# A two-layer graph kernel: statistics of two rows in one instruction, the mean taken off on GpSimd, the hidden layer of the edge weights computed in a stage of its own

## The chip, the cores and the metric

The kernel runs on one core of a Trainium2 chip. The metric is the device time of one execution in microseconds (us), without a profiler. The engines are TensorE (PE), VectorE (DVE), ScalarE (ACT), GpSimd (POOL) and SyncE (SP), which only issues transfers. Each runs its own instructions in order, and they wait for each other on semaphores.

## What is computed

100,000 nodes have 160 features each (64 scalars and 32 vectors of three), and 25,000 edges, sorted by their target, carry messages. Two layers follow each other, each with a layer norm and a ReLU ahead of it:

```python
h = jnp.maximum(_layernorm(x, axis=-1), 0.0)
x = x + L0(h, node_vec1, edge_attr_4, edge_attr_8, weights, src, dst)
h = jnp.maximum(_layernorm(x, axis=-1), 0.0)
x = x + L1(h, edge_attr_4, weights, edge_index)
```

In L0 every node gets a linear map of its own h, scaled by cos(angle). Every edge takes the mapped h of its source, times weights that a small network makes of the edge's 8 scalars, and the sums of the edges at a node go through a second map and are scaled by sin(angle). The small network is the part that the change moves:

```python
h = jax.nn.silu(edge_scalars @ fc_w1 * (1.0 / np.sqrt(8.0)))
weight = h @ fc_w2 * (1.0 / np.sqrt(64.0))
```

L1 gathers the rows of the sources again, forms messages, sums them per node, and adds the ReLU of a linear map of the sum. The layer norm's scale 1/sqrt(var + eps) is positive, so that the kernel takes the ReLU of x - mean first and multiplies by the scale later, behind the matmul.

## The kernel before

There are three stages behind a start of some 70 us, in which tables of the edges are computed and stored to DRAM.

**Stage 1** has 98 steps (u), one for each *unit* of 1024 nodes (8 rows in each of the 128 partitions). A step also handles two *tiles* of 128 edges; four tiles are a *quad* (q), so there are 49 quads of two steps each, an even one and an odd one. For a unit, DVE takes the statistics of the rows (`dense_stats`, L1334), forms mean and variance in small instructions (`moment_part`, L1203 to L1210) and takes the mean off 32 of the 160 columns (`rest_of`, L1215). ACT takes it off the other 128 with the ReLU (`dense_relu`, L763), PE transposes (L964, L965), ACT copies from PSUM (L770, L771), PE multiplies (`linear`, L969, L970), DVE scales and adds x (`dense_x1`, L1353) and takes the second statistics (L1362), ACT forms the second h (L755), and POOL adds it to x (`dense_y`, L625). POOL also computes the inverse roots by a power (`inverse_root`, L628). For a quad, POOL gathers the source rows with four indirect DMAs (L581), PE and ACT compute the hidden layer (`net_mm`, L1025; `net_silu`, L775), and DVE builds two selector matrices from a table of rows (`p1_selectors`, L1374). For a tile, PE multiplies (`p1_source`, ends with L1057), ACT copies (L802), DVE forms features (L1421, L1426, L1430), PE transposes them (L1083) and multiplies (L1043 to L1046), DVE forms the message (L1402, L1409), and PE sums (L1069, L1071).

SP's loop is a list of steps of its own (v). Step v loads the rows of unit v (`x_load`, L428). Even steps then load the source index (L443) and the edge scalars `q_sct` (L445) of quad v/2 + 1, and odd steps load the tables of quad (v-1)/2: `q_key`, `q_ed`, `q_row` (L450 to L452). Each step then stores the results of unit v-4 (L436, L438). DVE needs the tables of quad q at the end of its odd step 2q-1, so that SP has to be two steps ahead of DVE there.

**Stage 2** computes the 25,000 target rows again, with the edge sums, and scatters them to DRAM: per quad four indirect gathers and four indirect scatters on POOL, on DVE the same moments, an angle in eight small steps, and on ACT a Sine and two Square roots, which don't share a table. **Stage 3** handles layer L1's 196 tiles, with one indirect gather and one indirect scatter for each.

Of the kernel before, what the change touches and what calls it, by code (L numbers as in the profile page):

```python
# [19 lines left out]
P = 128  # L20
GD = 8
GQ = 4
# [52 lines left out]
def gnn_kernel(nc, xa, src, dst, number, edges_in, scalars_in, scalars_t_in, wpack, out):  # L75
# [19 lines left out]
    sum_tab = scratch("sum_tab", (Q, P, GQ * CW))  # L95
    y_tab = scratch("y_tab", (Q, P, GQ * D))
# [23 lines left out]
    with ExitStack() as ctx:  # L120
# [34 lines left out]
        minus_half = sb("minus_half", [P, GD])  # L155
# [21 lines left out]
        st1, st2 = four("st1", [P, GD, 6]), two("st2", [P, GD, 6])  # L177
        su1, su2 = four("su1", [P, GD, 2]), two("su2", [P, GD, 2])
        df1, df2 = four("df1", [P, GD]), two("df2", [P, GD])
        sq1, sq2 = four("sq1", [P, GD]), two("sq2", [P, GD])  # L180
        m21, m22 = four("m21", [P, GD]), two("m22", [P, GD])
        neg1, neg2 = four("neg1", [P, GD]), two("neg2", [P, GD])
        var1, var2 = four("var1", [P, GD]), two("var2", [P, GD])
# [16 lines left out]
        q_sct = two("q_sct", [GQ * SW, P])  # L200
# [5 lines left out]
        hr_e = two("hr_e", [P, GQ * 32])  # L206
# [9 lines left out]

        x_q = [x_all[:, i * GQ * XW:(i + 1) * GQ * XW] for i in range(4)]
# [4 lines left out]
        st_e = two("st_e", [P, GQ, 6])  # L222
        su_e = two("su_e", [P, GQ, 2])
        df_e = two("df_e", [P, GQ])
        sq_e = two("sq_e", [P, GQ])
        m2_e = two("m2_e", [P, GQ])
        neg_e = two("neg_e", [P, GQ])
        var_e = two("var_e", [P, GQ])
        sd_e = two("sd_e", [P, GQ])
        sd2 = two("sd2", [P, GQ])  # L230
# [38 lines left out]
        n_act = sem("net_hidden_ready")  # L269

        d_in = [sem(f"x_loaded{i}") for i in range(4)]
        d_ln1 = sem("dense_moments1")
        d_relu = sem("dense_h_ready")
# [6 lines left out]
        d_ln2 = sem("dense_moments2")  # L280
        d_h1 = sem("dense_h1_ready")
# [5 lines left out]
        e_tb = sem2("p1_tables_loaded")  # L287
        e_scl = sem("p1_scale_ready")
        e_g = sem2("p1_source_rows")
        e_ln = sem("p1_moments")  # L290
        e_relu = sem("p1_h_ready")
# [27 lines left out]
        r_relu = sem("p2_h_ready")  # L319
# [31 lines left out]
        def x3(t, w, g):  # L351
            return t[:, :].rearrange("p (g f) -> p g f", g=g, f=w)

# [14 lines left out]
        def _(sp):  # L368
# [53 lines left out]
            sp.wait_ge(s_rows, 32)  # L422
            sp.wait_ge(s_tab_out, 16 * n_out)
# [143 lines left out]
        def _(pool):  # L567
            nc.gpsimd.memset(t_next[:, :], N + 5).then_inc(s_fill, 1)
            nc.gpsimd.memset(t_prev[:, :], -1).then_inc(s_fill, 1)
            nc.gpsimd.memset(minus_half[:, :], -0.5)  # L570
# [40 lines left out]
            def p1_gather(q):  # L611
                j = q.mod(2)
                pool.wait_ge(e_ix[j], q.over(2, 16, 16))
                wait(pool, e_relu, q.times(1, -1))
                wait(pool, e_scl, q.times(2, -2))
                gather(xa, x_e[j], XW, i_src[j], e_g[j])
# [10 lines left out]
            def inverse_root(inv, var, n, signal):  # L627
                nc.gpsimd.tensor_tensor(inv[:, 0:n], var[:, 0:n], minus_half[:, 0:n], ALU.pow).then_inc(signal, 1)  # L628

            def dense_scale(u):  # L630
                j = u.mod(4)
                pool.wait_ge(d_ln1, u.times(5, 4))
                inverse_root(inv1[j], var1[j], GD, d_scl)
                pool.wait_ge(d_scl, u.times(2, 1))
                nc.gpsimd.tensor_tensor(scl1[j][:, :], inv1[j][:, :], x3(x_in[j], XW, GD)[:, :, D], ALU.mult).then_inc(d_scl, 1)

            def dense_norm2(u):
                j = u.mod(2)
                pool.wait_ge(d_ln2, u.times(4, 4))
                inverse_root(inv2[j], var2[j], GD, d_nmr)  # L640
                pool.wait_ge(d_nmr, u.times(2, 1))
                nc.gpsimd.tensor_tensor(nmr2[j][:, :], neg2[j][:, :], inv2[j][:, :], ALU.mult).then_inc(d_nmr, 1)  # L642

            def p1_scale(q):
                j = q.mod(2)
                pool.wait_ge(e_ln, q.times(5, 4))
                inverse_root(inv_e[j], var_e[j], GQ, e_scl)
                pool.wait_ge(e_scl, q.times(2, 1))
# [3 lines left out]
            def step(w):  # L652
                q = At(w.i, w.c // 2, 2)
                if w.mod(2) == 1 and (q + 1).within(Q):
                    p1_gather(q + 1)
                if (w - 1).within(U):
                    dense_scale(w - 1)
                if (w - 4).within(U):
                    dense_y(w - 4)
                if (w - 3).within(U):  # L660
                    dense_norm2(w - 3)
                if w.mod(2) == 0 and q.within(Q):
                    p1_scale(q)
# [3 lines left out]
            for w in range(8):  # L667
                step(At(0, w))
            with pool.Fori(2, U // 4) as i:
                for c in range(4):  # L670
                    step(At(i, c))
            for w in range(U - 2, U + 4):
# [74 lines left out]
        def _(act):  # L747
# [11 lines left out]
            def dense_relu(u, h):  # L759
                act.wait_ge(d_ln1, u.times(5, 3))  # L760
                x, hh = x_in[u.mod(4)], hb[u.mod(2)]
# [1080 lines left out]
```

## Time and profile before

| | us |
|---|---|
| Device time, median of three runs | 2476.07 (2475.62 to 2479.8) |
| Profiled execution, first to last instruction | 2863.6 |
| of it start, to 73 | 73 |
| stage 1, 73 to 1505 (49 quads) | 1432 |
| stage 2, 1505 to 2190 (49 quads) | 685 |
| stage 3, 2190 to 2863 (196 tiles) | 673 |

The profiled execution is 387 us longer than the kernel without a profiler. It is one execution, and each stage has a bound of its own: shares of the whole span say little. Durations of rows overlap a little: the next instruction of an engine can start before the one ahead is recorded as ended, so that the cost of one in a row of several is the distance of their starts.

### The profile page before, as it was taken

The numbers are of one execution on the slowest core, as the hardware profiler recorded it, in microseconds if no ns is written. First come the engines' busy times: TensorE is split into PE (matmuls) and PEld (weight loads), VectorE is DVE, ScalarE is ACT, GpSimd is POOL, SyncE is SP. The second block draws the span as 40 slices with busy tenths as digits, with TensorE's granted clock in tenths as the row PEclk, the third lists the DMA queues.
The fourth block names the chain that finished last, engine by engine and source line by source line (L and its number), as shares of the span: only waits on it lengthen the run. The fifth ranks groups of instructions, "written<-read, shape, count | busy, mean of one in ns | idle before, by whom it ended". The sixth has DMA issues, their size and how long they took to land.

```text
span 2863.6 us, 55863 instructions
## 1 busy us (share of the span) xinstructions
PE 1940.9 (68%) x12874; PEld 1820.7 (64%) x12874; DVE 1954.7 (68%) x8628; ACT 1560.1 (54%) x4412; POOL 1745.2 (61%) x1676
## 2 busy tenths in 40 slices
PE   0888888878878888878883343434344777777877
PEld 0777777777877777777773333323233777767777
DVE  2889888887888888888884655556555444444444
ACT  0667677776777777777774444545453222222222
POOL 1656666665666666766656565655565666666665
PEclk9989999998999999999995555555555999999898
DMA  9444544443444444454543232323332333333332
GB/s 79 142 143 169 172 170 171 172 172 138 169 172 170 173 169 164 162 179 147 180 154 124 87 89 87 93 87 97 88 99 83 81 89 88 92 92 90 94 95 74
DMA packets 223602, 364.52 MB, mean 127 GB/s; under 512 B 115938, under 2 KB 133149, under 8 KB 223405
## 3 DMA queue, kind: packets, MB, share of 16 engines
q1 hardware_dynamic: 176524, 289.81, 32.1%
q0 software_dynamic: 47040, 74.31, 9.8%
q14 instruction: 27, 0.21, 0.0%
q8 instruction: 11, 0.18, 0.0%
HBM read 176.85 MB, written 194.78 MB: 130 GB/s over the span
## 4 chain that ended last, share of the span: by engine, by line
DVE 31%; PE 25%; issue 14%; another core or an unknown queue 11%; POOL 8%; ACT 6%; SPq 2%; DMA 1%; DVEq 1%; ACTq 0%; POOLq 0%
DVE st L1334 3%; PE bank L969 3%; PE bank L1154 3%; POOL x_e L581 3%; POOL inv L628 3%; DVE x L1353 2%; DVE su_e L1203 2%; PE bank L964 2%; PE bank L1166 2%; DVE st L1362 2%; PE bank L1163 2%; ACT h L755 2%; PE bank L1176 2%; DVE x L1599 2%
## 5 line engine op out<-in xcount | busy, mean ns | idle before, releaser
L628 POOL TENSOR_TENSOR inv<-var,minus_half 128x8 f32<-128x8 f32 x196 | 327.7, 1672 | 256.5 <-DVE var L1210 253.4
L625 POOL TENSOR_TENSOR yo<-x,h 128x640 f32<-128x640 f32 x196 | 305.8, 1560 | 147.8 <-ACT h L755 145.4
L969 PE MATMUL bank<-wp,hT 128*128 128x160 f32 x1568 | 392.6, 334 | 1.6 <-DVE x L1353 0.7
L755 ACT ACTIVATE h<-x,nmr,inv 128x160 f32<-128x160 f32 x784 | 342.2, 514 | 6.1 <-POOL nmr L642 6.1
L587 POOL DMA_INDIRECT h_all<-h,i_put x196 | 203.4, 1038 | 217.9 <-ACT h L871 146.0
L964 PE MATMUL bank<-ident,h_e 128*128 128x128 f32 x392 | 83.0, 350 | 358.9 <-ACT h_e L878 229.2
L587 POOL DMA_INDIRECT out<-yo,i_put x196 | 202.1, 1031 | 197.2 <-DVE feat L1706 63.8
L1353 DVE SCALAR_TENSOR_TENSOR x<-bank,scl,x_all 128x160 f32<-128x160 f32 x784 | 254.3, 372 | 89.1 <-PE bank L970 46.0
L969 PE MATMUL bank<-wp,eT 128*128 128x160 f32 x784 | 274.5, 444 | 54.5 <-ACT eR L886 27.3
L934 ACT ACTIVATE tot<-bank 128x160 f32<-128x160 f32 x196 | 59.6, 304 | 455.7 <-remote 207.1
L964 PEld LDWEIGHTS bank<-ident,h_e 128*128 128x128 f32 x392 | 57.5, 184 | 367.9 <-DVE hr_e L1215 244.1
L1715 DVE TENSOR_TENSOR xr<-bank,q_ed 128x96 f32<-128x96 f32 x196 | 50.0, 255 | 334.0 <-PE bank L1166 175.6
L970 PEld LDWEIGHTS bank<-wp,hR 128*128 128x128 f32 x1568 | 268.4, 199 | 0.0
L970 PE MATMUL bank<-wp,hR 128*128 128x64 f32 x1568 | 268.4, 254 | 0.0
L581 POOL DMA_INDIRECT x_e<-in_xa,i_src x192 | 192.0, 1000 | 109.5 <-issue 48.0
L969 PEld LDWEIGHTS bank<-wp,hT 128*128 128x128 f32 x1568 | 253.0, 202 | 3.1 <-DVE x L1353 0.9
L763 ACT ACTIVATE hb<-x_all,neg 128x128 f32<-128x128 f32 x784 | 248.7, 394 | 0.0
L719 POOL DMA_INDIRECT h<-h_all,i_src x196 | 202.3, 1032 | 61.9 <-issue 58.4
L581 POOL DMA_INDIRECT x_all<-in_xa,i_dst x196 | 194.5, 992 | 65.6 <-issue 58.4
L1154 PE MATMUL bank<-ident,feat 128*128 128x128 f32 x784 | 136.1, 301 | 136.2 <-DVE feat L1706 109.8
L969 PEld LDWEIGHTS bank<-wp,eT 128*128 128x128 f32 x784 | 171.3, 270 | 73.8 <-issue 46.5
L964 PE MATMUL bank<-ident,hb 128*128 128x128 f32 x784 | 131.7, 294 | 117.7 <-ACT tot L810 115.9
(173 smaller groups left out, 6292.4 us busy)
## 6 DMA issues: line engine op xcount, KB each, us to landing
x_all<-in_xa SPq DMA_DIRECT2D x98, 644.0 KB, 5.8
h_all<-h SPq DMA_DIRECT2D x98, 640.0 KB, 2.9
out<-yo SPq DMA_DIRECT2D x98, 640.0 KB, 3.3
q_row<-row_tab SPq DMA_DIRECT2D x98, 256.0 KB
sum_tab<-tot SPq DMA_DIRECT2D x49, 322.0 KB, 4.2
y_tab<-yo SPq DMA_DIRECT2D x49, 320.0 KB
x<-y_tab SPq DMA_DIRECT2D x49, 320.0 KB
cv<-sum_tab SPq DMA_DIRECT2D x25, 322.0 KB
```

Source lines behind the costliest of these rows:

```text
L581: nc.gpsimd.indirect_dma_start(into[:, t * width:(t + 1) * width], None, rows, bass.IndirectOffsetOnAxis(ap=index[:, t:t + 1], axis=0)).th ...
L587: nc.gpsimd.indirect_dma_start(rows, bass.IndirectOffsetOnAxis(ap=index[:, t:t + 1], axis=0), tile, None, bounds_check=N - 1, oob_is_err=F ...
L625: nc.gpsimd.tensor_tensor(yo[j][:, a:b], x1[j][:, a:b], h1[j][:, a:b], ALU.add).then_inc(d_y, 1)
L628: nc.gpsimd.tensor_tensor(inv[:, 0:n], var[:, 0:n], minus_half[:, 0:n], ALU.pow).then_inc(signal, 1)
L719: nc.gpsimd.indirect_dma_start(h1[j][:, t * D:(t + 1) * D], None, h1_all, bass.IndirectOffsetOnAxis(ap=i_src[j][:, t:t + 1], axis=0)).then ...
L755: ins = nc.scalar.activation(h1[j][:, k * D:(k + 1) * D], x1[j][:, k * D:(k + 1) * D], ACT.Relu, bias=nmr2[j][:, k:k + 1], scale=inv2[j][: ...
L763: ins = nc.scalar.activation(hh[:, k * P:(k + 1) * P], x[:, k * XW + 32:k * XW + D], ACT.Relu, bias=neg1[u.mod(4)][:, k:k + 1])
L964: nc.tensor.transpose(ps_main[:, t * P:(t + 1) * P], main[:, t * P:(t + 1) * P], ident[:, :])
L969: nc.tensor.matmul(dst_ps, main[:, t * P:(t + 1) * P], wp[:, w:w + D], start=True, stop=False)
L970: return nc.tensor.matmul(dst_ps[:, 0:DS], rest[:, :], wp[:, w + D + t * DS:w + D + (t + 1) * DS], start=False, stop=True)
L1154: ins = nc.tensor.transpose(bank[n.mod(2)][:, c * P:(c + 1) * P], feat[n.mod(2)][:, c * P:(c + 1) * P], ident[:, :])
L1353: ins = V.scalar_tensor_tensor(x1[j][:, k * D:(k + 1) * D], bank[2 + pair % 2][:, k % 2 * D:(k % 2 + 1) * D], scl1[u.mod(4)][:, k:k + 1], ...
```

## The change

Four things are changed.

1. **Statistics.** One `bn_stats` instruction reads two rows, interleaved, and so puts out count, mean and squared deviation of each; the small instructions that joined the halves are gone. The roots are taken on ACT in stage 1 (for the nodes), with a reciprocal on DVE; for the edges POOL keeps its power.
2. **Mean.** The mean is taken off all 160 columns on POOL in stage 1 (`centre`), for a unit in an instruction of 1024 columns and one of 256, for a quad in one of 512 and one of 128. In stage 2 DVE does it.
3. **ReLU.** ACT's copy from PSUM applies it, and ACT's own instructions for it are gone.
4. **Hidden layer.** It is computed for all quads ahead of stage 1, in 13 groups of up to four quads, and stored to DRAM (`hid_tab`). In stage 1 SP loads it per quad, in the place of the scalars.

```diff
-    for k in range(GD):
-        ins = V.bn_stats(st1[j][:, k, :], x_in[j][:, k * XW:k * XW + D])
+    for pair in range(GD // 2):
+        ins = paired_stats(st1[j], pair, x_in[j], XW)
...
+def paired_stats(st, pair, rows, width):
+    two_rows = rows[:, 2 * pair * width:(2 * pair + 2) * width].rearrange("p (g f) -> p f g", f=width)
+    return V.bn_stats(st[:, 2 * pair:2 * pair + 2, :].rearrange("p g k -> p (g k)"), two_rows[:, 0:D, :])
...
+def centre(into, rest, rows, st, g, signal):
+    x = x3(rows, XW, g)
+    nc.gpsimd.tensor_tensor(x3(into, P, g), x[:, :, 32:D], bc_last(stat(st, g, 1), P), ALU.subtract)
+    nc.gpsimd.tensor_tensor(x3(rest, 32, g), x[:, :, 0:32], bc_last(stat(st, g, 1), 32),
+                            ALU.subtract).then_inc(signal, 1)
...
 def dense_copy(u, h):
-    nc.scalar.activation(hT[h][:, :], bank[0][:, :], ACT.Copy)
+    nc.scalar.activation(hT[h][:, :], bank[0][:, :], ACT.Relu)
...
 def p1_load(q):                       # SP
     j = q.mod(2)
     wait(sp, e_g[j], q.over(2, 64))
     sp.dma_start(i_src[j][:, :], src_tab[q.times(1)]).then_inc(e_ix[j], 16)
-    wait(sp, n_mm, q.times(1, -1))
-    sp.dma_start(q_sct[j][:, :], scalars_t[q.times(1)]).then_inc(n_in[j], 16)
+    wait(sp, e_pw, q.times(GQ, -GQ))
+    sp.dma_start(q_hid[j][:, :], hid_tab[q.times(1)]).then_inc(e_hid[j], 16)
...
+net_load(0)                            # SP, ahead of stage 1
+for g in range(NB):
+    if g + 1 < NB:
+        net_load(g + 1)
+    net_store(g)
+for j in range(2):
+    sp.wait_ge(n_st[j], 16 * ((NB + 1 - j) // 2))
```

The SP queue in the loop of stage 1: the end of an even step and the odd step behind it. `net_products_done` is the semaphore that `net_mm` counts, `p1_products_done` the one that `p1_source` counts, once for each tile. Before:

```order
L445 ISA [waits net_products_done]
L445 DMA q_sct<-scalars_t 32x128
L435 ISA
L436 ISA [waits dense_h1_ready]
L436 DMA h_all<-h 128x1280
L438 DMA out<-yo 128x1280 [waits dense_y_ready]
...
L428 DMA x_all<-in_xa 128x1288
...
L450 DMA q_key<-key_tab 128x8
...
L452 DMA q_row<-row_tab 128x512
```

In the changed kernel:

```order
L465 ISA [waits p1_products_done]
L465 DMA q_hid<-hid_tab 128x256
L455 ISA
L456 ISA [waits dense_h1_ready]
L456 DMA h_all<-h 128x1280
L458 DMA out<-yo 128x1280 [waits dense_y_ready]
...
L448 DMA x_all<-in_xa 128x1288
...
L470 DMA q_key<-key_tab 128x8
...
L472 DMA q_row<-row_tab 128x512
```

The transfers and their order are the same but for the hidden layer in the scalars' place; the wait ahead of it is another.

The POOL queue in the same loop. `inv`, `scl` and `nmr` are a unit's inverse root, its product with the node's attribute and the shift of the second norm, `yo` is the sum of x and h, and `hb` and `hr` are the rows less their mean. Before, the first step of the loop:

```order
L628 TENSOR_TENSOR inv<-var,minus_half 128x8 [waits dense_moments1]
...
L635 TENSOR_TENSOR scl<-inv,x_all 128x8 [waits dense_scale_ready]
...
L625 TENSOR_TENSOR yo<-x,h 128x640 [waits dense_out_stored0]
...
L625 TENSOR_TENSOR yo<-x,h 128x640 [waits dense_h1_ready]
...
L628 TENSOR_TENSOR inv<-var,minus_half 128x8 [waits dense_moments2]
```

In the changed kernel:

```order
L602 DMA x_e<-in_xa,i_src 128x161 [waits p1_centred]
L602 DMA x_e<-in_xa,i_src 128x161 x3
...
L649 TENSOR_TENSOR hb<-x_all,st 128x1024 [waits dense_h_transposed]
L650 TENSOR_TENSOR hr<-x_all,st 128x256
...
L645 TENSOR_TENSOR yo<-x,h 128x640 [waits dense_out_stored1]
...
L645 TENSOR_TENSOR yo<-x,h 128x640 [waits dense_h1_ready]
```

The roots have left POOL, two wide instructions stand ahead of the sums, and the gather has moved to the front of the even step.

## Rows read from the trace of the kernel before

**Rows 1.** Busy time by stage: busy us (x instructions), then clock, DMA share, GB/s

```profile
73.00:1505.00 1432.00, 1163.77 (x8272) 1096.56 (x8272) 1226.07 (x5217) 1034.31 (x3073) 928.50 (x871) 0.93 0.47 164
1505.00:2190.00 685.00, 262.50 (x1030) 234.90 (x1029) 398.23 (x2257) 338.69 (x745) 400.01 (x394) 0.52 0.31 93
2190.00:2863.00 673.00, 508.66 (x3528) 485.38 (x3528) 315.22 (x1078) 183.83 (x588) 407.21 (x395) 0.90 0.34 88
```

**Rows 2.** The chain that ended last, its shares by engine over the whole span

```profile
DVE 31%; PE 25%; issue 14%; another core or an unknown queue 11%; POOL 8%; ACT 6%; SPq 2%; DMA 1%; DVEq 1%; ACTq 0%; POOLq 0%
```

**Rows 3.** Timeline of POOL in stage 2: start, duration, instruction, [idle before]

```profile
1833.66 0.94 POOL L581 DMA_INDIRECT x_all<-in_xa,i_dst  x1 [0.30 <-issue]
1837.50 1.00 POOL L587 DMA_INDIRECT h_all<-h,i_put  x1 [0.30 <-issue]
```

**Rows 4.** Line L789, once in a quad: durations, first and last start

```profile
L789 ACT ACTIVATE eT<-bank x49: 597/597/597, 72.6 to 1465.9; 128x512 f32<-128x512 f32 x49
```

**Rows 5.** Groups by line and form: busy us, mean ns, idle before and releaser

```profile
L625 POOL TENSOR_TENSOR yo<-x,h 128x640 f32<-128x640 f32 x196 | 305.8, 1560 | 147.8 <-ACT h L755 145.4
L770 ACT ACTIVATE hT<-bank 128x512 f32<-128x512 f32 x196 | 117.0, 597 | 135.1 <-PE bank L965 133.5 <-issue 1.6
```

**Rows 6.** Timeline of POOL and DVE in an even step of stage 1

```profile
815.26 1.53 POOL L625 TENSOR_TENSOR yo<-x,h 128x640 f32<-128x640 f32 x1 [0.61 <-ACT h L755]
815.39 1.42 DVE L1206 TENSOR_SCALAR neg_e<-su_e 128x4 f32<-128x4 f32 x1
```

**Rows 7.** Busy time in stretches of 5 us in stage 1, columns as in rows 1

```profile
1110.00:1115.00 5.00, 3.87 (x31) 3.41 (x29) 3.68 (x16) 4.20 (x12) 3.57 (x4) 1.00 0.57 174
1120.00:1125.00 5.00, 4.38 (x19) 4.00 (x18) 4.12 (x13) 1.45 (x5) 1.18 (x1) 0.50 0.00 0
```

**Rows 8.** Timeline around a quad's selectors: SP, PE, DVE

```profile
817.43 0.35 SPq L428 DMA_DIRECT2D x_all<-in_xa  x1
819.46 0.33 SPq L452 DMA_DIRECT2D q_row<-row_tab  x1
828.15 0.95 PE L1057 MATMUL bank<-wp,q_hid 128*128 128x192 f32 x2
830.96 0.68 DVE L1374 TENSOR_TENSOR same<-q_row,q_key 128x512 f32<-128x512 f32 x1
```

**Rows 9.** Transfers of stage 1: count, KB each, median us from issue to landing

```profile
x_all<-in_xa SPq DMA_DIRECT2D x94, 644.0 KB, 5.8
sum_tab<-tot SPq DMA_DIRECT2D x48, 322.0 KB, 4.2
i_src<-src_tab SPq DMA_DIRECT2D x46, 2.0 KB, 5.2
```

**Rows 10.** Timeline of DVE and PE in stage 1, pieces of a step

```profile
817.39 1.25 DVE L1353 SCALAR_TENSOR_TENSOR x<-bank,scl,x_all 128x160 f32<-128x160 f32 x4
820.66 1.90 DVE L1334 BATCH_NORM_STATS2 st<-x_all 128x6 f32<-128x160 f32 x8
817.17 0.55 PE L1083 MATMUL bank<-ident,feat 128*128 128x128 f32 x3 [2.58 <-DVE feat L1430]
820.40 0.63 PE L964 MATMUL bank<-ident,hb 128*128 128x128 f32 x4 [0.59 <-ACT tot L810]
822.90 0.61 PE L964 MATMUL bank<-ident,h_e 128*128 128x128 f32 x4
851.59 0.61 PE L964 MATMUL bank<-ident,h_e 128*128 128x128 f32 x4
853.25 0.52 PE L1083 MATMUL bank<-ident,feat 128*128 128x128 f32 x3 [0.95 <-ACT eR L790]
```

**Rows 11.** Start: SP's last table store; a hidden layer on PE; transfers of 0:100

```profile
62.53 0.38 SPq L419 DMA_DIRECT2D row_tab<-t_row  x1
805.58 0.71 PE L1025 MATMUL bank<-q_sct,wp 32*128 32x128 f32 x4
q_sct<-scalars_t SPq DMA_DIRECT2D x4, 16.0 KB, 2.3
```

More of the change, by code:

```diff
@@ L205, in gnn_kernel @@
         h_e = sb("h_e", [P, GQ * P])
[L206 removed]
+        hr_e = sb("hr_e", [P, GQ * 32])
         part2 = two("part2", [P, GQ * D])
@@ L653, in step @@
                 q = At(w.i, w.c // 2, 2)
-                if w.mod(2) == 1 and (q + 1).within(Q):
[L655 to L663, printed above, removed]
+                if w.mod(2) == 0 and (q + 1).within(Q):
+                    p1_gather(q + 1)
+                if w.within(U):
+                    dense_centre(w)
+                if (w - 3).within(U):
+                    dense_y(w - 3)
+                if w.mod(2) == 1 and (q + 1).within(Q):
+                    p1_centre(q + 1)
+                    p1_scale(q + 1)
             pool.wait_ge(s_tab_in, 80)
             gather(xa, x_e[0], XW, t_src, e_g[0])
-            for w in range(8):
+            p1_centre(At(0, 0, 2))
+            p1_scale(At(0, 0, 2))
+            for w in range(4):
                 step(At(0, w))
-            with pool.Fori(2, U // 4) as i:
+            with pool.Fori(1, U // 4) as i:
                 for c in range(4):
                     step(At(i, c))
-            for w in range(U - 2, U + 4):
+            for w in range(U - 2, U + 3):
                 step(At(0, w))
@@ L831, in step @@
                 odd = u.mod(2) == 1
+                if (u - 2).within(U):
+                    dense_root2(u - 2)
                 if u.within(U):
-                    dense_relu(u, 0)
+                    dense_root1(u)
                 slot(u, 0)
-                if not odd and (q + 1).within(Q):
-                    net_silu(q + 1)
-                if odd and (q + 1).within(Q):
-                    p1_relu(q + 1)
                 if u.within(U):
@@ L851, in step @@
                     dense_h1(u - 2, 1)
-            net_silu(At(0, 0, 2))
-            p1_relu(At(0, 0, 2))
+            for g in range(-(-Q // GQ)):
+                net_silu(g)
             p1_copy(At(0, 0, 2))
@@ L873, in p2_h1 @@
                 ins.then_inc(r_h1, 1)
-            def p2_relu(q):
-                act.wait_ge(r_ln1, q.times(5, 3))
-                for t in range(GQ):
-                    ins = nc.scalar.activation(h_e[:, t * P:(t + 1) * P], x_q[q.mod(4)][:, t * XW + 32:t * XW + D],
-                                               ACT.Relu, bias=neg_e[q.mod(2)][:, t:t + 1])
-                ins.then_inc(r_relu, 1)
             def p2_copy(q):
@@ L1093, in slot @@
                 if (s - 1).within(T):
-                    p1_feat_t(s - 1, q1 if u.mod(2) == 0 and h == 1 and q1.within(Q) else None)
+                    p1_feat_t(s - 1)
                 if (s - 2).within(T):
@@ L1102, in step @@
             def step(u):
-                q = At(u.i, u.c // 2, 2)
-                odd = u.mod(2) == 1
                 slot(u, 0)
-                if not odd and (q + 1).within(Q):
-                    net_mm(q + 1)
                 if u.within(U):
@@ L1114, in _ @@
             pe.wait_ge(e_z, 1)
-            net_mm(At(0, 0, 2))
+            for g in range(-(-Q // GQ)):
+                net_mm(g)
+            pe.wait_ge(n_act, 2 * -(-Q // GQ))
             p1_tr(At(0, 0, 2))
@@ L1439, in step @@
                 rows = u.mod(2) == 0 and q1.within(Q)
+                odd = u.mod(2) == 1 and q1.within(Q)
                 if now:
                     dense_x1(u - 1, 0)
+                if (u - 2).within(U):
+                    dense_inverse2(u - 2)
+                if now:
                     dense_x1(u - 1, 1)
+                if (u - 2).within(U):
+                    dense_shift2(u - 2)
+                if now:
                     dense_stats2(u - 1, 0)
```

300 lines of the change are left out of this document (129 added, 171 removed).

## The prediction

> **What bounds the kernel now.** I read the stages first, since the shares of the whole span mix them. In [rows 1], stage 1 takes 1432 of 2863 us and keeps DVE busy for 1226 and PE for 1164; stages 2 and 3 take 685 and 673 us with no engine over 76%. The chain of waits [rows 2] gives DVE 31% and PE 25%, and 11%, 315 us, to a source that none of the kernel's work explains. Most of that sits in stages 2 and 3, and the profiled execution is 387 us longer than the median: I take those gaps for the profiler's own. What bounds these two stages without it is POOL's queue. An indirect transfer occupies it for 0.94 or 1.00 us and 0.30 to the next [rows 3], 1.27 on average. Stage 2 has eight per quad, 49 x 8 x 1.27 = 498 us, stage 3 two for each of 196 tiles, another 498; with filling and draining, some 1010 together. The median then leaves 2476 - 73 - 1010 = 1393 us for stage 1, **28.4 us per quad**. The trace has (1465.9 - 72.6)/48 = 29.0 [rows 4]. The median is the time that I sum against, and 28.4 is how it divides; against the span, the same differences would stand on 2863.6.
>
> **What the change takes out of stage 1, per quad.** *ACT* loses 16 of the rows' ReLUs and four for the edges, 20 x 0.3 (a copy of 512 columns has 0.6 [rows 5], these have 128), 6 us, and gains four roots of 0.2. It is off the path in most steps. *DVE* loses 36 statistics instructions for 18; eight take 1.90 [rows 10], 0.23 each, of which some 0.17 are its 160 columns at one per cycle; a pair as one instruction saves about 0.06, 1.1 us in all. The lower bound for the new one is 0.23, if two interleaved rows went at double rate, the upper 0.5 or more, if the stride cost something; I take 0.39, since nothing in the trace shows strided columns to be slower. It also loses 33 small instructions, some 3.2 us, and gains eight, 0.6. And it loses a stall: `neg_e` has four columns and took 1.42 us, ending with POOL's sum that started just ahead of it [rows 6]; there are two of these in most quads, 2.4 us. DVE is lighter by 6 of some 25 us. *PE* loses the hidden layer, 0.6 us [rows 11], but at that place it covers a wait of 0.59 for ACT's copy [rows 10], so that nothing is won. *POOL* trades its roots for wide differences: a sum of 640 columns takes 1.56 [rows 5], so 1280 columns take some 3.1 us per unit; with the edges' 640 and their scale the quad's POOL work stays at 21 us, gather included. Bounds for the 1280 columns: 2 us, if a broadcast operand is cheaper, 6 if twice as dear; 3.1 is by the nearest row, the same instruction.
>
> If nothing else changed, the longest loop would be POOL's: from DVE's statistics of an odd unit through difference (3.1), sum (3.1), the edges' difference and scale (3.3), gather (5.8), difference (3.1) and half a sum (1.5) back to DVE, and 4.9 there: 24.8 us; PE needs 23 to 24 with its unavoidable waits. Such loops ran 28.4 where the engines' sum was 25, so some 26.5 would come of it.
>
> **A wait that is added.** SP's `p1_load(q+1)` in its even step now waits until `p1_source` is through with quad q-1, since the buffer `q_hid` is read until then. Before, it waited for a product finished long before. The wait ends when PE has done its second tile of step 2q-1. Queued behind it on SP are the stores of unit 2q-4, the load of unit 2q+1 and the **tables of quad q**, which DVE needs for the selectors at the end of the same step 2q-1. [Rows 8] show the distance: `q_row` was issued at 819.46 and the selectors began at 830.96, 11.5 us later, hence without a wait. But `p1_source`, whose last product is L1057, ended at 828.15 + 0.95 = 829.1, 1.9 us ahead of the selectors. In the changed kernel the seven transfers start only there. From that end to the issue of `q_row`: from `x_all` to `q_row` it is 2.0 us [rows 8], and `q_hid` and two stores ahead take 0.5 each with the wake-up, 3.9 in all. The data wait behind 2 MB: the load of x lands 5.8 us after its issue, and even 2 KB issued behind it take 5.2 [rows 9]. `q_row` lands between 3.9 + 2.3 = 6.2 us (small loads of the start [rows 11]) and 10 us (x at 1.9 + 5.8, its own 256 KB and the stores ahead). I take 9.0, nearer to [rows 9], since these stand in the same queue.
>
> The quad is then a ring. After the landing: selectors 1.2; DVE's first half of a step 3.4 (817.39 to 820.66 [rows 10], less the pair's gain, plus two small ones), the next unit's statistics 1.6, two pairs of `x1` 1.2, statistics 1.6, features and message 1.2, small ones 0.2 and one stall behind POOL's difference, 1.0: 10.2. Then PE, by starts in [rows 10]: features to the next transposes 3.2 (817.17 to 820.40), these and the products 2.5 (to 822.90), the edges' transposes with ACT's copy 1.7 (851.59 to 853.25), and to the end of `p1_source` 2.1: 9.5. Sum 9.0 + 1.2 + 10.2 + 9.5 = 29.9. In the ring PE idles for some 2 us behind the tables. The granted clock fell to 0.50 in 1120:1125 after such a gap [rows 7], with 1.00 shortly before; I add 0.6. **30.5 us per quad, 49 x (30.5 - 28.4) = +103 us.** Bounds: 27 with the earliest landing and no loss, 33 with the latest and a fall of the clock in each quad.
>
> **The stage of its own.** SP's queue is full of table stores until 62.5 [rows 11], and the loads come behind them: nothing hides the stage. For a group, PE has two products of 512 columns. Four records of 128 columns took 0.71 [rows 11], and four of 512 take at least 2 us, twice that at the lower clock. The loop of two groups on the same buffers goes over a store (322 KB landed in 4.2 us [rows 9]; these are 512), the load behind it, a product and a copy of 0.6 [rows 5]: 7.5, or 3.7 per group. 12.25 groups are 46 us, and filling and the last store, less what stood there before, add 2: **+48 us** (30 if only PE counts, 67 if load and store follow each other).
>
> **Stages 2 and 3.** In stage 2 the statistics shrink and DVE takes the mean off 160 columns, where ACT did 128. Both lie beside POOL's eight transfers, 10.2 us per quad, against 8.3 for DVE's quickest. If that cover were gone, DVE would be the bound and lighter by a microsecond. I count nothing, and in the profile some tens of microseconds less, since fewer instructions wait for a semaphore there. Stage 3 is untouched.
>
> Sum: 2476 + 103 + 48 = 2627; I say **2625 us**.
>
> **Rivals.** *A. The ring above*: 2625. *B. The tables come in time*, and the lighter engines count: 26.5 per quad, -93 + 48, **2431 us**. It needs a landing after 5 us (21.5 + 5), below my lower bound, or PE to run further ahead of DVE than the 1.9 us of [rows 8]. For it: in other quads PE led by as little, but DVE becomes lighter, not PE, which speaks against. It is even with the kernel before at 27.4 per quad, a landing after 5.9 us; the low end of A, 27, is already past that point. *C. The port that POOL and DVE share.* The stall of [rows 6] is the mechanism: POOL would be in such an instruction for 15 of 26 us in longer pieces (2.4 us), and DVE has some nine instructions with two SBUF operands in a quad, at about 0.6 each 5 us, of which my sum has 1 in the path. With the ring, 2.5 more per quad: 33, 49 x 4.6 + 48, **2749 us**. The Trainium skill states the rule (SBUF — State Buffer, Who interferes with whom): a DVE instruction with two SBUF inputs and a GpSimd one that reads SBUF exclude each other for their whole length; by that rule the trace agrees, 1.42 us against the 0.16 of its like. *D. The change does less than it says*: two interleaved rows cost as much as two instructions. That is 1 us per quad in DVE's part, inside the range.
>
> **How the numbers follow.** A 0.65, of it 0.05 at its low end where it is faster and 0.05 within the bound; C 0.16; B 0.19. A measurement can tell some 0.2%, 5 us, so a result within that of 2476 means no change. Faster 0.24, same 0.05, slower 0.71. The range takes in B's upper half and C up to its middle: 2435 to 2730.
>
> **What would show it.** In the profile after: DVE idle ahead of the selectors on `q_row`, once per quad, some 7 us (if not, A falls); `q_row` issued behind the end of the tile's last product; quads of some 30 us; a stretch of 45 to 50 us between table stores and the first step with PE, ACT and SP in it; DVE's busy share in stage 1 down from 86% to about 65%; POOL's differences at 2.4 and 0.7 us. Quads of 26 to 27 us would make the prediction wrong, and so would stages 2 and 3 that change without the profiler.

## The result, and the profile after

| | median us (runs) | profiled span |
|---|---|---|
| before | 2477.94 (2475.62 to 2483.44) | 2863.6 |
| after | 2717.62 (2716.09 to 2722.42) | 2715.7 |

The ratio is 1.0973, with a 95% interval of 1.0955 to 1.0991: the changed kernel is 240 us slower. The profiled execution of after took what its runs take, so its rows can be read as they stand; that of before had been 387 us longer than its runs. First the stages, in the columns of [rows 1].

```profile
115.00:1650.00 1535.00, 1183.08 (x8080) 1103.32 (x8080) 1216.29 (x3130) 816.96 (x2251) 870.82 (x831) 0.91 0.45 160
1650.00:2187.00 537.00, 269.69 (x1068) 241.83 (x1069) 362.03 (x1537) 291.00 (x547) 411.48 (x397) 0.55 0.40 117
2187.00:2715.00 528.00, 451.07 (x3491) 443.91 (x3489) 314.89 (x1065) 181.59 (x580) 396.96 (x381) 0.95 0.40 108
```

Stage 1 has grown. Stages 2 and 3 look 290 us shorter than in [rows 1], but only because those carried the gaps of one execution; what they cost in runs is measured below. The line that answers [rows 4], and the chain of waits that answers [rows 2]:

```profile
L814 ACT ACTIVATE eT<-bank x49: 597/597/597, 112.3 to 1598.4; 128x512 f32<-128x512 f32 x49
...
PE 28%; DMA 16%; issue 16%; DVE 16%; SPq 8%; ACT 7%; POOL 6%; DVEq 1%; POOLq 0%; ACTq 0%
```

The first quad starts at 112.3 instead of 72.6, and quads follow each other at (1598.4 - 112.3)/48 = 31.0 us. In the chain DVE fell from 31% to 16% and DMA rose from 1% to 16%. Three groups of the page say where to look (busy us, mean ns, idle before and its releaser):

```profile
L649 POOL TENSOR_TENSOR hb<-x_all,st 128x1024 f32<-128x1024 f32 x98 | 187.7, 1915 | 465.2 <-DVE st L1210 464.1
L1427 DVE TENSOR_TENSOR feat<-feat,q_ed 128x96 f32<-128x96 f32 x196 | 296.6, 1513 | 0.0
L1379 DVE TENSOR_TENSOR same<-q_row,q_key 128x512 f32<-128x512 f32 x98 | 68.0, 693 | 322.2 <-DMA q_row<-row_tab 322.1
```

The selectors wait for `q_row`. The 322 us of the page take in stage 3; stage 1 alone has this:

```profile
L1379 DVE TENSOR_TENSOR same<-q_row,q_key x49: 681/692/694, 120.0 to 1602.8; 128x512 f32<-128x512 f32 x49
...
  DMA q_row<-row_tab: 249.1, 48
```

Of these 249 us 82 stand once at the start, which leaves 3.5 per quad. And L1427, a product of 96 columns, takes 1513 ns on average. In the kernel before, its like took 269.

**The ring**, on SP, PE and DVE (it answers [rows 8]):

```profile
818.97 0.54 PE L1069 MATMUL bank<-wp,q_hid 128*128 128x192 f32 x2
...
819.69 0.33 SPq L465 DMA_DIRECT2D q_hid<-hid_tab  x1
...
821.32 0.78 SPq L448 DMA_DIRECT2D x_all<-in_xa  x1
...
824.35 0.44 SPq L472 DMA_DIRECT2D q_row<-row_tab  x1
...
829.74 0.69 DVE L1379 TENSOR_TENSOR same<-q_row,q_key 128x512 f32<-128x512 f32 x1 [3.72 <-DMA q_row<-row_tab]
```

PE ends `p1_source` at 819.5, SP wakes at 819.7, and with the two stores and the load of x in front `q_row` is issued at 824.35. The selectors begin at 829.74, 10.2 us after PE's end; over 45 quads of stage 1 the median is 10.4.

**A hold**, on POOL and DVE (it answers [rows 6]):

```profile
820.43 1.93 POOL L649 TENSOR_TENSOR hb<-x_all,st 128x1024 f32<-128x1024 f32 x1
822.30 0.63 POOL L650 TENSOR_TENSOR hr<-x_all,st 128x256 f32<-128x256 f32 x1
822.89 3.01 POOL L645 TENSOR_TENSOR yo<-x,h 128x640 f32<-128x640 f32 x2
...
820.75 5.28 DVE L1427 TENSOR_TENSOR feat<-feat,q_ed 128x96 f32<-128x96 f32 x1
```

L1427 reads two tensors from SBUF. Begun 0.3 us after POOL's centring, it ends with POOL's run of four instructions, at 826.0. About one in four is caught so (mostly 5.3 to 6.1 us), the others take 0.24. The Trainium skill (SBUF — State Buffer, Who interferes with whom) lets such a DVE instruction and a reading GpSimd instruction exclude each other for one instruction's length; here the trace goes further, since the wait lasts through four.

**The stage of its own**, on SP and PE:

```profile
59.22 0.38 SPq L418 DMA_DIRECT2D row_tab<-t_row  x1
...
62.65 7.16 PE L1040 MATMUL bank<-yo,wp 32*128 32x512 f32 x8 [43.61 <-DMA yo<-scalars_t]
70.44 7.19 PE L1040 MATMUL bank<-yo,wp 32*128 32x512 f32 x8 [0.63 <-DMA yo<-scalars_t]
...
110.91 1.12 PE L979 MATMUL bank<-ident,h_e 128*128 128x128 f32 x4 [0.37 <-ACT x L806]
```

Two groups (eight records) come every 7.8 us, 3.9 per group. PE is busy for 7.2 of it and waits 0.6 for the load, so that PE bounds the stage.

So there were three candidates for 240 us: the ring, the hold and the stage, and one unknown, how the runs of before divide between the stages.

### The profile page after: what moved, and what is told of

The parts are those of the page before. It is cut to its first block, busy times and chain, and to the rows that moved or that the text cites. A ratio compares the mean times of both kernels' runs of the same rounds, so it can differ in the third digit from the quotient of the medians.

```text
span 2715.7 us, 51496 instructions
## 1 busy us (share of the span) xinstructions
PE 1953.1 (72%) x12730; PEld 1807.0 (67%) x12730; DVE 1906.1 (70%) x5786; ACT 1308.1 (48%) x3409; POOL 1687.4 (62%) x1628
## 4 chain that ended last, share of the span: by engine, by line
PE 28%; DMA 16%; issue 16%; DVE 16%; SPq 8%; ACT 7%; POOL 6%; DVEq 1%; POOLq 0%; ACTq 0%
DMA q_row<-row_tab 10%; PE bank L984 5%; DVE feat L1427 4%; POOL h_all L608 3%; ACT h L777 3%; DMA x_all<-in_xa,i_dst 3%; DVE st L1210 3%; PE bank L1093 2%; PE bank L985 2%; PE bank L979 2%; DVE x L1353 2%; DMA out<-yo,i_put 2%; PE bank L1069 2%; POOL x_all L602 2%; PE bank L1056 2%
## 5 line engine op out<-in xcount | busy, mean ns | idle before, releaser
L649 POOL TENSOR_TENSOR hb<-x_all,st 128x1024 f32<-128x1024 f32 x98 | 187.7, 1915 | 465.2 <-DVE st L1210 464.1
L984 PE MATMUL bank<-wp,hT 128*128 128x160 f32 x1568 | 403.1, 341 | 12.9 <-DVE x L1353 12.3
L645 POOL TENSOR_TENSOR yo<-x,h 128x640 f32<-128x640 f32 x196 | 298.8, 1532 | 98.1 <-ACT h L777 98.0
L1427 DVE TENSOR_TENSOR feat<-feat,q_ed 128x96 f32<-128x96 f32 x196 | 296.6, 1513 | 0.0
L1379 DVE TENSOR_TENSOR same<-q_row,q_key 128x512 f32<-128x512 f32 x98 | 68.0, 693 | 322.2 <-DMA q_row<-row_tab 322.1
L1353 DVE SCALAR_TENSOR_TENSOR x<-bank,scl,x_all 128x160 f32<-128x160 f32 x784 | 254.1, 365 | 17.0 <-PE bank L985 16.3
L1093 PE MATMUL bank<-ident,feat 128*128 128x128 f32 x588 | 110.0, 299 | 205.4 <-DVE feat L1427 157.6
L608 POOL DMA_INDIRECT h_all<-h,i_put x196 | 215.3, 1098 | 61.5 <-issue 58.6
L798 ACT ACTIVATE hT<-bank 128x512 f32<-128x512 f32 x196 | 117.0, 597 | 226.6 <-PE bank L980 226.6
L1093 PEld LDWEIGHTS bank<-ident,feat 128*128 128x128 f32 x588 | 67.8, 153 | 228.4 <-DVE feat L1427 170.5
L1210 DVE BATCH_NORM_STATS2 st<-x 128x6 f32<-128x320 f32 x490 | 218.0, 485 | 0.0
```

Of the source, the lines that this page charges most:

```text
L608: nc.gpsimd.indirect_dma_start(rows, bass.IndirectOffsetOnAxis(ap=index[:, t:t + 1], axis=0), tile, None, bounds_check=N - 1, oob_is_err=F ...
L645: nc.gpsimd.tensor_tensor(yo[j][:, a:b], x1[j][:, a:b], h1[j][:, a:b], ALU.add).then_inc(d_y, 1)
L984: nc.tensor.matmul(dst_ps, main[:, t * P:(t + 1) * P], wp[:, w:w + D], start=True, stop=False)
L1093: ins = nc.tensor.transpose(bank[4][:, c * P:(c + 1) * P], f[:, at:at + P], ident[:, :])
L1210: return V.bn_stats(st[:, 2 * pair:2 * pair + 2, :].rearrange("p g k -> p (g k)"), two_rows[:, 0:D, :])
L1353: ins = V.scalar_tensor_tensor(x1[j][:, k * D:(k + 1) * D], bank[2 + pair % 2][:, k % 2 * D:(k % 2 + 1) * D], scl1[u.mod(4)][:, k:k + 1], ...
```

## The experiments

All times are medians beside runs of the kernel before on the same chip (2480 to 2486 us). "Pace" is the start of the 49th `same` less that of the first, over 48, in the profile of that run. "Rest" is the median less the start of the 49th.

| kernel | us | ratio to before (95%) | pace | rest |
|---|---|---|---|---|
| before, stage 1 only | 1424.6 | | 27.2 | |
| after | 2717.6 | 1.097 (1.096 to 1.099) | 30.9 | 1115 |
| after, `q_hid` loaded behind the tables | 2693.5 | 1.086 (1.084 to 1.088) | 30.1 | 1132 |
| after, no two SBUF inputs in features | 2747.0 | 1.108 (1.106 to 1.110) | 31.3 | 1123 |
| after, both | 2523.7 | 1.018 (1.016 to 1.020) | 26.8 | 1119 |
| before + stage and its wait | 2825.0 | 1.138 (1.135 to 1.141) | 33.3 | 1106 |
| before + stage, `q_hid` behind the tables | 2528.6 | 1.020 (1.018 to 1.021) | 27.1 | 1109 |
| hidden layer in the loop | 2604.8 | 1.051 (1.048 to 1.054) | 29.6 | 1115 |
| the same, no two SBUF inputs in features | 2476.4 | 0.998 (0.997 to 0.999) | 26.9 | 1118 |
| and selectors ahead of `dense_stats` | 2419.2 | 0.973 (0.971 to 0.975) | 25.7 | 1111 |
| and selectors while POOL gathers | 2400.9 | 0.965 (0.962 to 0.968) | 25.2 | 1120 |
| in the loop, gather between centre and sum | 2417.7 | 0.973 (0.971 to 0.974) | 25.5 | 1121 |
| in the loop, features mended, gather last | 2559.3 | 1.030 (1.028 to 1.033) | 28.6 | 1115 |

**1. How before divides.** On every engine all that follows stage 1 is left out, so that nodes with edges lack the second layer.

```diff
-    p2_step(...) and p3_slot(...) with their loops, on SP, POOL, ACT, PE and DVE
+    SP waits for the last stores of h, out and sum_tab
```

> The kernel before with stages 2 and 3 left out (the rows of touched nodes get no second layer). It gives the time of the start and stage 1 without a profiler. The prediction's split (73 us of start, 28.4 per quad) gives about 73 + 1393 + 12 for the last stores: about 1475 us. The split by the profile after (stages 2 and 3 cost 1100 us there) gives 2478 - 1100 = about 1380 us, 26.6 per quad.

1424.6 us, between the two. Its profiled span is 1422.5, 2 us less than its run, so that it has none of the gaps that made the profile of before longer:

```profile
L1067 DVE TENSOR_TENSOR same<-q_row,q_key x49: 675/680/693, 71.0 to 1374.6; 128x512 f32<-128x512 f32 x49
```

Stage 1 of before runs at 27.2 us per quad and not at 28.4. Behind the 49th selectors 2480 - 1375 = 1105 us follow, in all other kernels 1106 to 1132: the change does little to stages 2 and 3, some 10 us more.

**2. The wait, in the changed kernel.**

```diff
     i_src load
-    wait(sp, e_pw, ...); q_hid load      # p1_load(q + 1), even step
 ...
     q_key, q_ed, q_row loads             # p1_tables(q), odd step
+    wait(sp, e_pw, ...); q_hid load      # for q + 1
```

> The changed kernel, except that SyncE issues the load of q_hid for the next quad behind the three table loads of this quad, instead of ahead of them. Theory W (the wait on e_pw, with the tables queued behind it, sets the pace of stage 1: 30.9 us per quad in the profile after against about 26.6 without it): 48 quads get 4.3 us back, 2717 - 206 = about 2510 us. Theory P (GpSimd's centring holds up VectorE's feature instructions, 1513 ns for the 96-column one against 269, and that sets the pace): the pace stays near 30, 2670 us or more.

Only 24 us came back (2693.5). By itself that would speak for theory P.

**3. The stage and its wait in the kernel before.** Statistics, ReLUs and roots stay as they were.

```diff
-    net_mm(q + 1), net_silu(q + 1)       # in the even step of PE and ACT
+    net_mm(g), net_silu(g)               # all groups ahead of the first step
-    wait(sp, n_mm, ...); q_sct load      # p1_load(q + 1)
+    wait(sp, e_pw, ...); q_hid load
```

> The kernel before with the hidden layer alone changed: computed in a stage of its own, q_hid loaded by SyncE behind the same wait on e_pw; statistics, mean and ReLU as before. Theory W: it gets the wait and the stage, so 2478 + 43 for the stage + about 4.3 x 48 = 206: about 2725 us, or a little more since VectorE's half of the ring is longer in this kernel. Theory P: no centring on GpSimd, so nothing but the stage: 2478 + 43 = about 2520 us.

2825.0: 345 us slower, more than the whole change. The pace went to 33.3, and every selector waited:

```profile
L1400 DVE TENSOR_TENSOR same<-q_row,q_key x48: 691/692/693, 119.0 to 1691.3; 128x512 f32<-128x512 f32 x48
...
  DMA q_row<-row_tab: 431.9, 48
```

Its counterpart has the same stage with `q_hid` behind the tables:

> The kernel before with the hidden layer in a stage of its own, but q_hid loaded by SyncE behind the table loads, so that no table waits for e_pw. No centring on GpSimd. If the wait is the whole of what before plus the stage lost besides the stage itself: 2480 + 43 = about 2525 us (2505 to 2545). If reading q_hid from memory or the later start of the loop costs something else: 2600 us or more.

2528.6. The wait alone, without any centring on POOL, is 2825 - 2529 = **296 us**, and the stage alone **47 us**. The selectors have no wait but the one at the start:

```profile
L1406 DVE TENSOR_TENSOR same<-q_row,q_key x49: 676/681/693, 116.8 to 1419.8; 128x512 f32<-128x512 f32 x49
...
  DMA q_row<-row_tab: 78.7, 1
```

**4. The statistics without the stage.** The changed kernel with two products and one SiLU per quad in the loop, as before; the diff is that of experiment 3 with + and - exchanged.

> The changed kernel with the hidden layer back in the loop (two products and one SiLU per quad, inputs loaded by SyncE behind n_mm) and no stage of its own; statistics, centring, ReLU in the copy and roots as in the changed kernel. Theory W: no wait and no stage, so the time of before or a little less for VectorE's and ScalarE's 6 us per quad: 2430 to 2480 us. Theory P: the centring on GpSimd alone makes a quad dearer by 3 to 5 us: 2620 to 2700 us.

2604.8: 125 us slower than before with no wait and no stage. That is theory P's outcome, 15 us below the near end of its 2620 to 2700: both theories hold. Its features, written without two SBUF inputs:

```diff
-    tensor_tensor(f[128:320], w[128:192] (x3), g[64:160], mult)
+    tensor_tensor(f[128:224], w[128:160] (x3), g[64:160], mult)
 ...
-    tensor_tensor(f[224:320], f[224:320], ed(j, t, 1, 4), mult)
+    for i in range(3):      # w is in PSUM, the scalar is a column
+        scalar_tensor_tensor(f[224 + i::3], w[160:192], ed(j, t, 1 + i, 2 + i), g[64 + i::3], mult, mult)
```

> The changed kernel with the hidden layer back in the loop, and VectorE's features written so that no instruction of them reads two tensors from SBUF: the 96-column product feat x q_ed becomes three products of 32 columns (PSUM x a column of q_ed x g_e), and the 192-column product becomes one of 96. Theory P (an instruction with two SBUF inputs is held until GpSimd's run of centring and addition ends, once per quad, 5.3 us, and PE waits 2.9 us of it for the features and 1.2 behind that): with the hold gone 2.9 to 4.1 us x 48 come back, 2605 - 140 to 195 = 2410 to 2465 us. Theory L (the centring is simply one more step between statistics and transposes, and its latency sets the pace): 2580 us or more.

2476.4: the hold had cost 128 us here, 2.7 per quad, where PE's waits in the profile had led me to expect 2.9 to 4.1. The 128 us include what a lower clock cost, see below.

**5. Both causes, taken apart in the changed kernel.**

> The changed kernel whole (the stage, the wait on e_pw ahead of the tables), with the features written without two SBUF inputs. If the ring through q_row holds the pace by itself, as in before plus the stage, the hold lies under the wait for q_row and nothing comes back: 2690 to 2717 us. If the hold is the larger part of the 240 us: below 2600 us.

2747.0: nothing came back, it is even 29 us slower, 30 beyond the forecast's end. The pace accounts for 21 of the 29 (31.3 against 30.9, 0.4 us in 48 quads), the rest stands behind the 49th quad. Three narrow products in place of one take longer for DVE (0.58 against 0.24 us a tile, with 0.10 won back on the product ahead of them); whether that is the 0.4 was not tested. Every selector waits again, 479 us in all with the 83 of the start, 8.3 per quad:

```profile
L1379 DVE TENSOR_TENSOR same<-q_row,q_key x49: 689/693/694, 120.5 to 1624.0; 128x512 f32<-128x512 f32 x49
...
  DMA q_row<-row_tab: 479.4, 48
```

> The changed kernel with q_hid loaded behind the tables and with the features written without two SBUF inputs. If the ring and the hold are the whole story in stage 1, this is the loop version without the hold plus the price of the stage: its time + 43, so 2455 to 2510 us. If either alone still binds: 2600 us or more.

2523.7. Here are the four together, with the stage in all of them:

| | wait ahead of the tables | wait behind them |
|---|---|---|
| two SBUF inputs | 2717.6 | 2693.5 |
| mended | 2747.0 | 2523.7 |

Taking one cause away gives 24 or -29 us, taking both gives 194. The two don't add: each is a loop of its own, 31 us per quad through the tables and 30 through the hold, and the longer sets the pace. In after it is the ring, with the hold 1 us behind it. The waits say the same. In after DVE is held for 5.1 us per quad (four tiles, 1.51 less 0.24) and then waits 3.5 for `q_row`, 8.6 together; without the hold it waits 8.3. A study that had mended only one would have called it harmless.

**The clock in these numbers.** The experiments change a third thing with the two causes: the granted clock of TensorE. Stage 1 from the first to the 49th selectors in after, with both mended, and in before with stage 1 only, columns as in [rows 1]:

```profile
120.00:1602.80 1482.80, 1152.52 (x7853) 1074.70 (x7854) 1189.14 (x3053) 790.08 (x2176) 845.34 (x810) 0.91 0.45 159
...
118.00:1405.00 1287.00, 1042.04 (x7856) 965.51 (x7857) 1173.72 (x3437) 788.53 (x2176) 846.20 (x812) 1.00 0.53 183
...
71.00:1374.60 1303.60, 1089.18 (x8058) 1025.52 (x8059) 1177.89 (x5111) 1006.02 (x2998) 896.96 (x854) 0.97 0.51 177
```

PE has the same work in the first two and is busy for 24.0 us per quad in after, for 21.7 with both mended. In after the clock falls to 0.50, the lower of its two levels, in 45 stretches, 273 us together; with both mended it does so once, for 3.4 us. In the quad of the traces above PE idles for 2.8 us until DVE's held features come at 826.0. The stretch at 0.50 begins at 827.3, and `p1_source`'s last product takes 0.95 us in it, 0.54 a tile earlier:

```profile
818.97 0.54 PE L1069 MATMUL bank<-wp,q_hid 128*128 128x192 f32 x2
...
826.08 0.55 PE L1093 MATMUL bank<-ident,feat 128*128 128x128 f32 x3 [2.76 <-DVE feat L1427]
...
827.93 0.95 PE L1069 MATMUL bank<-wp,q_hid 128*128 128x192 f32 x2
```

Quads with and without such a stretch differ in length. With stage 1 only, the 22 quads that hold one take 29.6 us, the 26 others 25.1. In the version in the loop with the hold, 36 quads take 30.2 and the 12 without a stretch 27.6; with the features mended no stretch is left, and the pace is 26.9. Which part of 296, of 128 or of 194 us is the wait itself, and which the lower clock that comes with it, no run separates.

**6. Where DVE's saving went.** With both mended or with neither present the pace is 26.8 or 26.9, only 0.3 below before's 27.2, though DVE has 4.6 us less to do (busy for 24.5 us per quad with stage 1 only, for 20.0 in the last version of this section, where no wide instruction is held). And before's 27.2 is a mean over quads at a lower clock; at full clock it runs 25.1, faster than this. The version in the loop with mended features shows why:

```profile
818.61 5.31 DVE L1373 TENSOR_TENSOR same<-q_row,q_key 128x512 f32<-128x512 f32 x1
...
817.88 1.92 POOL L642 TENSOR_TENSOR hb<-x_all,st 128x1024 f32<-128x1024 f32 x1
819.75 0.62 POOL L643 TENSOR_TENSOR hr<-x_all,st 128x256 f32<-128x256 f32 x1
820.33 3.03 POOL L638 TENSOR_TENSOR yo<-x,h 128x640 f32<-128x640 f32 x2
```

The hold has moved to the selectors, which also read two tensors from SBUF: 46 of the 49 are held, and the mean is 4.8 us instead of 0.68. Three ways to get them out of it. One puts them ahead of `dense_stats` in the even step, where POOL waits for DVE:

```diff
     p1_features(s0, 2)
+    if u.mod(2) == 0 and tile: p1_selectors(q)
     dense_stats(u + 1)
...
-    if odd: p1_selectors(q1)             # end of the step
```

> The loop version without two-SBUF features, and VectorE's two selector comparisons of a quad moved from the end of the odd step to just before dense_stats in the even step, where GpSimd has nothing to run since it waits for exactly those statistics. In the profile without the move, same<-q_row,q_key takes 5.31 us instead of 0.68 behind GpSimd's run, once per quad, and VectorE is busy 91% of stage 1. Theory P2 (the hold moved from the features to the selectors, and VectorE, held, still sets the pace): the pace falls from 26.9 to 22.5 to 25 us per quad, 2476 - 90 to 215 = 2260 to 2385 us. Theory M (the pace of 26.9 is set by PE, ScalarE and GpSimd, and the hold is slack): 2465 to 2485 us.

2419.2: 57 us back, 34 short of the nearer end of what theory P2 gave. The next puts them ahead of the outer product in the odd step, where POOL issues its gather:

```diff
     p1_stats(q1)
+    if odd: p1_selectors(q1)
     p1_outer(s1 - 2)
...
-    if odd: p1_selectors(q1)             # end of the step
```

> As the former, but the selectors stand in the second half of the odd step, ahead of the outer product, while GpSimd issues its gather of four indirect DMAs (817.88 us is where its next operation on data begins, VectorE is there at 815.9). Theory P2: issuing DMAs doesn't hold VectorE, so the comparison takes about 0.7 us there, and the time falls as in the former, 2260 to 2400 us, unless q_row has not landed 3 us earlier. Theory M: 2465 to 2485 us. If issuing indirect DMAs holds VectorE too: no better than 2440.

**2400.9 us**, 3.5% faster than the kernel before, the best of all. The selectors now take 0.67 beside POOL's indirect transfers, in all but two of the 49 quads:

```profile
827.40 0.67 DVE L1373 TENSOR_TENSOR same<-q_row,q_key 128x512 f32<-128x512 f32 x1
...
833.65 0.68 DVE L1347 SCALAR_TENSOR_TENSOR x<-bank,scl,x_all 128x160 f32<-128x160 f32 x2 [3.57 <-POOL yo L638]
```

Both came out at or beyond the slow end of their forecasts because of the second row: DVE is no longer held, but waits for POOL's sum, which comes behind the gather and the centring (3.6 us here, 164 in all of stage 1, 3.4 per quad). The third way leaves DVE alone and breaks POOL's run:

```diff
+    dense_centre(w)
     p1_gather(q + 1)        # even step
-    dense_centre(w)
     dense_y(w - 3)
```

> The changed kernel with the hidden layer in the loop, its features and selectors as the change has them (two SBUF inputs), and one change of order on GpSimd: the gather of the source rows is issued between dense_centre and dense_y of the even step, so that centring and addition no longer stand in one run of 5.3 us. Theory P (an instruction with two SBUF inputs is held until the run ends): the longest hold falls to 2.5 to 3 us, and 2605 falls by 2.3 to 2.8 us per quad to 2465 to 2495 us. If the hold comes of each GpSimd operation by itself and not of the run, or doesn't set the pace: within 20 us of 2605.

2417.7, 187 us less than the version it was made from, where I had expected at most 140. One moved line of POOL frees the features, and the selectors too, since DVE comes to them during the gather.

```profile
834.64 0.25 DVE L1421 TENSOR_TENSOR feat<-feat,q_ed 128x96 f32<-128x96 f32 x1
834.81 0.68 DVE L1373 TENSOR_TENSOR same<-q_row,q_key 128x512 f32<-128x512 f32 x1
...
834.39 0.95 POOL L595 DMA_INDIRECT x_e<-in_xa,i_src  x1 [0.30 <-issue]
```

**7. A miss.** To take the wait for `yo` away as well, the gather was put last in the even step, with mended features and the selectors in their old place.

```diff
-    p1_gather(q + 1)        # even step
     dense_centre(w)
     dense_y(w - 3)
+    p1_gather(q + 1)
```

> The loop version with features without two SBUF inputs and the selectors where the change has them (end of the odd step), and on GpSimd the even step issues its gather last, behind dense_centre and dense_y. In the profile of the version with the selectors in the gather, a quad takes 24.9 us, of which VectorE waits 3.6 us for yo (GpSimd's addition, which stands behind 5 us of gather), and VectorE is busy 19.9 us, PE 21.7. Theory Y (what is left is yo queued behind the gather): the addition ends 5 us earlier, the selectors meet no run on GpSimd, and the pace goes to what PE needs with its waits, 22.5 to 24 us: 2401 - 45 to 120 = 2280 to 2355 us. Theory Z (the gather issued 5 us later brings x_e too late for p1_stats, which then waits): 2400 us or more. If the hold on the selectors is back (run of 5.5 us just ahead of them): about 2450.

2559.3. By the number that is theory Z's "2400 or more", but its mechanism isn't there: DVE waits for `x_e` once, 1.9 us. The hold has found a third instruction, the scale of eight columns (0.15 when free, more than 1 us longer in 46 of 96 cases), and POOL's sum now keeps the gather waiting for ACT's `h`:

```profile
814.13 1.54 POOL L638 TENSOR_TENSOR yo<-x,h 128x640 f32<-128x640 f32 x1 [5.45 <-ACT h L770]
...
820.69 1.92 POOL L642 TENSOR_TENSOR hb<-x_all,st 128x1024 f32<-128x1024 f32 x1
822.56 0.62 POOL L643 TENSOR_TENSOR hr<-x_all,st 128x256 f32<-128x256 f32 x1
823.14 1.53 POOL L638 TENSOR_TENSOR yo<-x,h 128x640 f32<-128x640 f32 x1
...
820.56 4.15 DVE L1337 TENSOR_TENSOR scl<-inv,x_all 128x8 f32<-128x8 f32 x1
```

POOL waits 285 us for `h` in this stage, against 64 in the best version. The clock falls to 0.50 in 30 stretches, against one; the quads without such a stretch take 26.7 us, against 25.0. How much of the 158 us over the best version is the scale, the wait for `h` or the clock was not taken apart.

## Why the prediction was right, and what was mis-sized

The forecast was 2625 us by rival A, the ring; measured were 2718, inside the range. By the number alone that is nearer to rival C's 2749; that it is A, and not C, rests on experiment 5, where the hold taken out gives nothing back. Step by step:

- **The division of before** is the term that was furthest off. I took POOL's queue for the bound of stages 2 and 3 and added little for filling and draining: 1010 us, which left 28.4 us per quad. The kernel with stage 1 alone gives 27.2, and 2480 - 1425 = 1055 for what follows. The ring was therefore measured against a base 1.2 us too high: 49 x 1.2 = 59 of the 93 us that were missing. A bound from one queue is a lower bound; I had used it as the time. The 387 us of gaps I put into stages 2 and 3 for the most part; some 95 of them were in stage 1 (29.1 us per quad in that profile against 27.2).
- **The ring**: 30.5 was forecast, 31.0 measured, 0.5 x 49 = 24 us. Of its pieces the landing was short: 9.0 from PE's end to the selectors, 10.2 in the trace. Most of that is SP, which issued in 4.8 instead of 3.9 (`q_key` and `q_ed` take 1.09 and 0.68 us to issue there); from the issue of `q_row` to the selectors it is 5.4, where the forecast had 5.1. Large transfers landed later than before, x_all after 7.6 us and `sum_tab` after 7.0, against 5.8 and 4.2 in [rows 9]. The rest of the ring is 20.8 against 21.5. In it I had 0.6 us for a fall of the clock. The fall came in nearly every quad, and PE is busy for 2.3 us per quad more than with both mended. How much of that lies in the ring, and so whether the 0.6 was too small and another piece too large, is open.
- **The stage**: +48 forecast, 47 measured in two pairs of kernels (2523.7 - 2476.4, 2528.6 - 2481.8). By group, 3.9 against 3.7, and that is in part luck: I had put the store and load loop at its bound, and it was PE, which took 3.6 us for the four records of a group, near the "twice that" which the prediction gave for the lower clock.
- **Stages 2 and 3**: nothing forecast, some 10 us measured.
- **Rival C, the hold**, was a real mechanism and had the wrong arithmetic. I added 2.5 us per quad to the ring for it. By itself it costs 2.7 (29.6 against 26.9), but DVE is held while it would wait for the tables anyway, so in after it costs nothing. It belonged to a loop of its own, and the time there is 2605 without the stage and 2694 with it, not 2749. The idle time ahead of the selectors, 3.5 us per quad instead of the 7 I named, is the other side of this: without the hold it is 8.3, and in the kernel without centring on POOL 7.3. And the row of [rows 6] that I set beside the rule is not a case of it: `neg_e` reads one tensor from SBUF, not two, and is held all the same. L1427 above, with two, is one.
- **Rival B**, tables in time: forecast 26.5 per quad, measured 26.8. Its 2431 us were wrong mostly by the base again (59 of 93): 2523.7. My sum of POOL's loop (24.8) missed that the lighter DVE is held for 4.6 us at the selectors; with that gone, 25.2 to 25.7 were reached.
- **DVE's saving**: 6 us forecast, 4.6 measured where no wide instruction is held.
- **Small terms**: the paired statistics are 0.41 us for two rows (1.69 for eight, forecast 0.39). The centring takes 1.92 and 0.63 where I had 2.4 and 0.7. DVE's busy share in stage 1 is 79% and not 65%, the difference being the hold, which is counted as busy: without it the changed kernel has 66% (20.6 of 31.3 us).

## What to carry to other kernels

A wait in a queue costs what stands behind it, not what it guards: here a load needed a quad later stopped the tables needed at once, and it is worth 296 us where nothing else covers it, what the lower clock added included. Compare the granted clock of two versions before a difference is put down to a wait alone. When two suspects are loops of their own, test them together as well as singly, since the second is invisible until the first is gone. Moving wide elementwise work to POOL makes every DVE instruction with two SBUF inputs a possible wait as long as POOL's whole run; break the run with work that only issues, or place such instructions beside it.

## What was new of the hardware

- A held DVE instruction can wait through several POOL instructions: 5.28 us through four at L1427, 5.31 at the selectors, 4.15 at a scale that began 0.13 us ahead of POOL's first. The same scale, begun in the middle of the centring, was let through at that instruction's end (0.97 us). What decides between the two was not tested. DVE instructions with one input in PSUM ran beside POOL at their usual time (L1353 of after, 0.32 to 0.39 in all 760 cases), and so did the selectors, with two in SBUF, while POOL only issued indirect transfers (0.67).
- Two inputs in SBUF are not the whole class. `neg_e` in the kernel before has one tensor input and one constant, and 19 of its 48 instructions in stage 1 are held, up to 1.54 us, and end with an instruction of POOL. The reciprocals of after, with one input too, take 0.17 to 0.21 in all cases, 95 of them wholly beside an instruction of POOL. Why the one is held and the other not was not tested.
- PE ran the stage and its first work behind it at half its later rate. The four transposes at 110.91 (above) took 1.12 us and started 0.21 apart, those at 127.44 take 0.67 and start 0.11 apart. In the stage, records of 512 columns start 0.85 apart, 0.21 per 128 columns. The clock's column (third from the end) says 1.00 there, but that is no reading: the trace's first clock record stands at 127.6 us, and the column prints 1.00 where it has none. In all the traces here the first record comes 5 to 9 us behind the first selectors, so that no trace tells the clock of the start. What the halving is due to was not tested.

```profile
127.44 0.67 PE L979 MATMUL bank<-ident,hb 128*128 128x128 f32 x4
...
62.00:70.00 8.00, 7.16 (x8) 2.49 (x8) 0.00 (x0) 1.94 (x4) 0.00 (x0) 1.00 0.23 74
```

- POOL's difference of 1024 columns with a broadcast operand took 1.92 us, less per column than the sum of 640 without one (1.53).
- The profiled execution of before was longer than its runs also in stage 1 (29 us per quad against 27.2), and those of all other kernels were not. Why that one was, stays open; a kernel that keeps a single stage gave the division that the profile could not.
